# First graph layer: its aggregation cut into four pieces that stand between the outer-product groups of the next pair of destination tiles

## What is computed

```
def gin_layer(x, src, dst, ew, w1, b1, w2, b2):
    msg = x[src] * ew[:, None]
    agg = jax.ops.segment_sum(msg, dst, num_segments=x.shape[0])
    h = agg + x
    h = jax.nn.relu(h @ w1 + b1)
    return h @ w2 + b2
```

## Time and profile before

| | |
|---|---|
| runs, median (lowest to highest) | 4908.68 us (4903.77 to 4911.19) |
| profiled execution | 4919.42 us, span 4917.9 us |
| busy over the span | PE 2780.7 us, DVE 2375.0, ACT 595.5, POOL 2781.4 |
| outer products L857 | 4992 matmuls, 191.6 us |
| loads of one-hot operands on DVE: L1267, L1268, L1271 | 104, 104 and 312 instructions |
| granted clock of PE, mean over the span | 0.709 |

### The profile page before, as it was taken

The page is one execution under the profiler, slowest core; times in us unless marked ns, Lnnn a source line. Parts: engine busy times, 40 slices in busy tenths (PEclk is TensorE's granted clock), DMA queues, the critical chain, the costliest instruction groups (busy, mean ns, idle before and its releaser), DMA issues. The chain is left out here.

```text
span 4917.9 us, 62825 instructions
## 1 busy us (share of the span) xinstructions
PE 2780.7 (57%) x13804; PEld 1994.1 (41%) x13804; DVE 2375.0 (48%) x7342; ACT 595.5 (12%) x1968; POOL 2781.4 (57%) x2942
## 2 busy tenths in 40 slices
PE   0666679962665655556666555565654444444444
PEld 0555456541343433344444433343443333333333
DVE  5766644134455555555345555555533333333332
ACT  2111113001200000000220000000021000000001
POOL 2000002023777777777277777777727777777773
PEclk9777689986777777877787777777775555555555
DMA  3122226540444444444244444444423222222222
GB/s 68 62 88 89 89 103 261 185 153 21 102 109 109 109 109 109 108 109 109 40 103 109 108 109 109 108 109 109 108 38 55 56 57 56 57 56 57 56 56 21
DMA packets 246378, 451.12 MB, mean 92 GB/s; under 512 B 163276, under 2 KB 165074, under 8 KB 241469
## 3 DMA queue, kind: packets, MB, share of 16 engines
q0 software_dynamic: 122928, 318.15, 27.6%
q1 hardware_dynamic: 111150, 128.71, 7.8%
q10 hardware_dynamic: 12144, 2.18, 0.2%
HBM read 392.00 MB, written 57.21 MB: 91 GB/s over the span
## 5 line engine op out<-in xcount | busy, mean ns | idle before, releaser
L494 POOL DMA_INDIRECT rows_all<-gat_tab,ell x2664 | 2516.9, 945 | 820.8 <-issue 624.8
L998 PE MATMUL banks<-rows_all,ident 128*128 128x264 f32 (+1 forms) x5328 | 1801.2, 507 | 1559.0 <-PEq L118 1559.0
L998 PEld LDWEIGHTS banks<-rows_all,ident 128*128 128x128 f32 x5328 | 1303.0, 285 | 2056.4 <-issue 1869.3
L1570 DVE COPY lrel<-m_all 128x8 f32 x666 | 147.9, 222 | 1527.5 <-DMA rows_all<-gat_tab,ell 1198.8
L1595 DVE TENSOR_TENSOR rows_all<-rows_all,banks 128x1024 f32<-128x1024 f32 (+1 forms) x666 | 685.0, 1042 | 136.4 <-DVE ex_in L1583 136.4
L787 ACT ACTIVATE banks<-ex_in 128x40 f32<-128x40 f32 x666 | 138.3, 208 | 3076.4 <-ACTq L118 3076.4
L494 POOL DMA_INDIRECT edges<-sw_d,edge_pick x28 | 34.6, 1235 | 510.6 <-POOLq L118 498.5
L857 PE MATMUL banks<-rows_all 128*128 128x52 bf16 x4992 | 191.6, 204 | 213.9 <-PEq L118 207.9
L1548 DVE TENSOR_TENSOR acc<-acc,banks 128x264 f32 (+1 forms) x675 | 259.3, 384 | 43.8 <-DVEq L118 11.7
L857 PEld LDWEIGHTS banks<-rows_all 128*128 128x128 bf16 x4992 | 181.1, 109 | 232.9 <-issue 232.6
L1541 DVE TENSOR_TENSOR acc<-acc,banks 128x264 f32 (+1 forms) x675 | 259.7, 385 | 5.2 <-DVE acc L1548 4.6
(11 more groups left out here) (276 smaller groups left out, 2223.7 us busy)
## 6 DMA issues: line engine op xcount, KB each, us to landing
rows_all<-gat_tab,ell POOLq DMA_INDIRECT x2664
x_t<-adj_d SPq DMA_DIRECT2D x11, 3328.0 KB, 11.0
y_t<-adj_d SPq DMA_DIRECT2D x11, 3328.0 KB, 10.8
adj_d<-x_t SPq DMA_DIRECT2D x7, 3328.0 KB, 9.8
adj_d<-y_t SPq DMA_DIRECT2D x6, 3328.0 KB, 11.1
ell<-ell_d SPq DMA_DIRECT2D x666, 2.5 KB
acc<-key_d SPq DMA_DIRECT2D x1, 1664.0 KB, 6.3
acc<-vec_d SPq DMA_DIRECT2D x1, 1664.0 KB, 21.0
```

Source lines behind the costliest of these rows:

```text
L494: return g.indirect_dma_start(out=dst, out_offset=None, in_=table, in_offset=bass.IndirectOffsetOnAxis(ap=idx, axis=0))
L998: last = t.matmul(sum_ps[u % SUMS][:, 0:width], ident[:, :], rows[u][:, r * width:(r + 1) * width], start=(r == 0), stop=(r == SLOTS - 1))
L1570: v.tensor_copy(lrel[:, SLOTS, :], plane(m_all[:, now, :]))
```

## The change

The aggregation of the pair before, which stood in one piece between the parts 1 and 2, is cut into four: source tiles 0 to 6 behind part 1, 7 to 13 behind part 2, 14 to 19 behind part 3, 20 to 25 behind part 4. The hidden product stands behind part 5 and the output product behind part 6 (before: ahead of part 3 and ahead of part 5). ACT's copies move to the same places, and `keep_hidden` on DVE moves from ahead of group 7 to behind it.

```diff
--- before.py
+++ after.py
@@ -67,8 +67,9 @@
 PART_AT = 64
 PART_W = GROUP_DST * PAIR * T
 WEIGHT_PARTS = 3
-AGG_AT, MID_AT, TURN_AT, OUT_AT = 2, 3, 4, 5
-MASK_AT, NEXT_AT, OUT_KEPT_AT = 2, 6, 7
+AGG_AFTER = {1: (0, 7), 2: (7, 14), 3: (14, 20), 4: (20, T)}
+TURN_AT, MID_AFTER, OUT_AFTER = 4, 5, 6
+MASK_AT, NEXT_AT = 2, 6
 PAIR_ORDER = {1: [12, 11, *range(0, 11)], 2: [9, 10, *range(0, 9), 11, 12]}
 LISTED_AT = {i: range(*(t * T // 10 for t in (i - 3, i - 2))) for i in range(3, PAIRS)}
 PAIR_HOME = {1: [i % 2 for i in range(PAIRS)], 2: [(i + 1) % 2 for i in range(PAIRS)]}
@@ -708,11 +709,11 @@
                 for c in range(GROUPS):
                     if c == 0:
                         take(act, adj_stored[u], 16)
-                    if c == AGG_AT and not first:
+                    keep_part(u, c)
+                    if c == max(AGG_AFTER) and not first:
                         keep_agg(1 - u)
-                    if c == MID_AT and not first:
+                    if c == MID_AFTER and not first:
                         keep_mid(0)
-                    keep_part(u, c)
 
             act.wait_ge(weights_landed, 16 * WEIGHTS)
             keep_pair(0, first=True)
@@ -881,16 +882,17 @@
                 for c in range(GROUPS):
                     if c == TURN_AT:
                         turn_edges(1 - u)
+                    part(c, part_made[c % PART_RING])
                     if not first:
-                        if c == AGG_AT:
+                        if c == min(AGG_AFTER):
                             pe.sem_inc(adj_made, 1)
                             take(pe, own_ready)
-                            aggregate(h_own, h_in, 1 - u, 1 - u, 0, T)
-                        if c == MID_AT:
+                        if c in AGG_AFTER:
+                            aggregate(h_own, h_in, 1 - u, 1 - u, *AGG_AFTER[c])
+                        if c == MID_AFTER:
                             gin_hidden(0)
-                        if c == OUT_AT:
+                        if c == OUT_AFTER:
                             gin_out(0)
-                    part(c, part_made[c % PART_RING])
                 with pe.If(more > 0):
                     with pe.Fori(0, more):
                         turn_edges(2)
@@ -1293,9 +1295,9 @@
                                     else deg_all[:, bass.ds((k + 1) * PAIR + j, 1)])
                     if c == NEXT_AT:
                         split_sources(1 - u)
-                    if c == OUT_KEPT_AT and not first:
-                        keep_hidden(k - 1, h_mid)
                     one_hot(u, c)
+                if not first:
+                    keep_hidden(k - 1, h_mid)
                 link.reset()
                 mores = dve.value_load(mores_i[0:1, of_pair_at(k)], min_val=0, max_val=PAIRS * BLOCKS)
                 with dve.If(more > 0):
```

## The result

The changed kernel takes 4834.3 us (median of 4 runs, 4829.1 to 4838.3), the kernel before 4909.9 us beside it. The ratio is 0.9849, interval 0.9837 to 0.9861: 75.7 us less, where 87 were forecast, and inside the range (the forecast was 4822 us). The second layer's first product (own rows of `h_mid`) starts at 703.85 us before and at 624.93 us after, so the stretch of the pairs gave 78.9 us. (The two profiled executions differ by 90.4 us in their spans. 11.5 us of that lie behind this point, 4214 us against 4203; over the profiles of the first and the third set of experiments this part varies from 4204 to 4213 us, 4204 in a repeat of the change, so it is the spread of the later layers. The start of the second layer varies too from one profile of a kernel to the next: by 1.9 us for the changed kernel, by 0.5 and 7.4 us for two others that were profiled twice.)

The account below looks back on a forecast made before the run. Bound: PE and DVE waiting for each other in the pair blocks, through a ring of two. Saving 7 x 6.5 + 5 x 8.5 = 88 us, less 1, from the median: 4908.7 - 87 = 4822 us; 8-in-10 range 4798 to 4862.

Parts of the forecast that it names:

- DVE and PE wait for each other because of the ring of two: Pair blocks: two one-hot buffers cannot bridge 12.5 us of matmuls; DVE's 146.7 us of waits fall to some 50.
- The walk through a pair: One pair laid end to end on PE and DVE: period 35.4 us without the jump, 39.0 with it.
- The sum: Twelve pairs: 7 x 6.5 + 5 x 8.5 = 88 us saved, less 1 us for the first pair.
- the price of keep_hidden behind G7: End of a pair on DVE: keep_hidden takes 1.2 us behind group 7, covered by PE's branch.
- P7 at the full clock from 0.3 to 1.7: PE's matmuls on the last group, from 0.3 to 1.7 us after DVE finishes that group, at full clock.
- The prediction's own sign of being wrong: At the branch behind part 7: prediction wrong if PE's gap grows once that part ends sooner.
- PE doesn't get its clock back: Rival, aggregation in pieces: PE's clock stays at 0.50, pairs 47.7 and 52.0 us, +63 us, 4972; chance 0.04.
- DVE alone as the bound: Rival, pair loop: DVE's own 32.2 us a pair, 1.4 more at a jump, sets the time; 138 us saved, 4771; chance 0.04.
- Later layers pass the gain on: Last aggregation and two later layers: PE's own chain, all moved forward, so the 87 us pass through to the end.

Follow-up runs that it names:

- the first and the third set of experiments: First: keep_hidden moved alone, four pieces alone, keep_hidden one pair later, two pieces (kernel before 4912.5 us). Third: change repeated, dummy products, a fifth piece, loop written out (4909.5).
- five pieces: Changed kernel with keep_hidden one pair later, aggregation in five behind parts 1 to 5, hidden and output products behind parts 6 and 7: 4797.7 us against 4909.5 before.
- the filled wait: Changed kernel plus six unused dummy products in PE's wait ahead of part 6: 4844.3 us against 4909.5 for the kernel before.

## Why the prediction was nearly right, and what it missed

The sign, the mechanism and the places were right, the saving was 11 us (13%) smaller than forecast. By its own steps:

- *DVE and PE wait for each other because of the ring of two* holds as far as the length of a piece goes: two pieces give 9 us, four 76, the wait of 9 us is gone, and DVE's waits ahead of its groups are 49.8 us where some 50 were forecast. The ring itself was not changed.
- *The walk through a pair.* Own rows to P2: 4.95 us forecast, 4.8 measured in the pair shown (345.77 to 350.57), 3.9 to 5.6 and 4.9 in the mean over all. P2 to P7: 19.5 forecast, 19.9 measured. P7 to the own rows without a jump: 11.0 forecast, 11.8 to 12.1 measured (11.0 in the first pair). With a jump: 14.5 forecast, 14.9 to 15.9 measured.
- *The sum.* The seven periods without a jump are 36.7 us in the mean where 42.0 were before, 5.3 less, and the five with one 39.8 against 48.1, 8.3 less: 37 + 42 = 79 us. Forecast were 6.5 and 8.5. So nearly the whole miss lies in the pairs without a jump, 7 x 1.2 us. That the 8.5 came out so well is luck in part: the walk had the period with a jump too short as well (39.0 us, measured 39.8), but the kernel before takes 48.1 us there in the mean, where the prediction reckoned with 47.4 to 47.8. The remaining 3 us, 75.7 in the medians against 79 in the profiles, are in the spread of the later layers.
- *The step that failed* is the price of keep_hidden behind G7: 1.2 us and covered by PE's branch. It brings 1.49 us of idle DVE with it that the walk didn't have, since in the earlier trace rows DVE goes on at 368.56 without any idle time. G0 ends that much later and part 0 with it, and PE's branch covers this at a jump alone: without one P0 starts 3.53 us behind the start of G0 in six of the seven pairs, as soon as G0's results are there. That makes 0.8 of the 1.2 us a pair; some 0.4 us are in the walk from P2 to P7. Taking keep_hidden off that place gave 2.8 us in each pair without a jump and nothing in the others, 18.5 us in the stretch of the pairs and 13 us in the time.
- *P7 at the full clock from 0.3 to 1.7* was wrong as well: it took 2.24 us in every pair, because the clock fell while P6 ran (in three of the twelve pairs of the loop) or just behind it (P6 took 1.37 us in the other nine). The wait ahead of P6 is 1.88 us, longer than the 1.2 to 1.6 us over which the clock had held before; the prediction said that no wait would be longer, while its own walk had PE wait from 30.8 to 32.6 there. Without a jump this cost nothing, since DVE set the start; with one it cost at most some tenths (P0 behind P7's start: 9.6 us with five pieces, 10.2 in the changed kernel), and the filled wait won nothing back. The prediction's own sign of being wrong, a gap at the branch that grows once P7 ends sooner, was seen there: 9.0 to 9.4 us at a jump in place of 7.5 to 8.5.
- *PE doesn't get its clock back*, the rival on the other side, is refuted: the clock is back in the first piece, every P2 to P5 of the pair shown runs in 1.38 us. The Trainium skill (TensorE: Matmul & The Clock Gate, HAM oscillation) warns of an engine that waits between bursts and starts each of them cold. The trace agrees for P0, P1 and the start of the first piece (2.24, 2.24 and 3.96 us) and for P7, and not for the pieces after it.
- *DVE alone as the bound* was not reached by the change. It needed keep_hidden in another place, a fifth piece and no jump; then the time is 4772.5 us where the rival had 4771. That these two agree so closely is chance: the rival's sum kept the jumps, with 1.4 us of DVE at each.
- *Later layers pass the gain on* holds: the third layer and the first gathers of `rec_d` start 79.0 us sooner, the first product of the attention layers (`gat_w`) 83.0 us (1228.5 and 1145.5).

## What to carry to other kernels

Where two engines hand work to each other through a ring of n buffers, put other work of one of them between the groups in pieces of about the length of a group; cutting it once may give almost nothing (9 of 76 us here). Before moving a short instruction that waits for its own predecessor to the end of a loop's body, ask what the engine's queue did under the long instructions that stood there: the branch and the register load were hidden under them. Read the price of a jump on the engine that takes longest over it, and for pairs with and without a jump apart: twice here a small sum was the difference of two effects of some 10 us. And when the head of a loop is set by another engine, a faster last instruction ahead of the branch buys nothing.

## What I had not expected of the hardware

The branch over the unused loop and the jump back hold PE's queue for 3.3 to 4.3 and 4.6 to 5.0 us in the changed kernel, more than the 48 matmuls of a part; around the jump at 370.45 us the first lasts from 371.75 to 375.58 and the second from 375.75 to 380.77, and P0 follows at 381.09. The Trainium skill (Runtime: NRT & Kernel Launch, Instruction fetch mechanics) says that a taken branch breaks the sequential fetch, and that the code of its target is then fetched by a DMA. The trace agrees: among the DMA packets of the kind `instruction` one of 16384 bytes runs inside the first of these branches (373.30 to 374.24 us), and two inside the second (from 376.66 and 376.82, the last ends at 378.67). The same branch over the unused loop is not always as long: 3.84 us in the median of the changed kernel, 4.46 with the filled wait, for which no run gives the reason. Writing the loop out gained 25 us of time although that branch stayed in every pair.
